# Row sums of an integer softmax on GpSimd, one activation table for Ln and Exp, and a longer run of filler transposes

## The reference, cut to what matters

```python
def _int_log2_softmax(x, scaling_factor):
    ...
    exp_int = jnp.maximum(jnp.floor(z * 2.0 ** (n - q)), 0.0)
    exp_sum = exp_int.sum(axis=-1, keepdims=True)
    ratio = jnp.round(exp_sum / jnp.maximum(exp_int, 1.0))
    ...
    rounds = _log_round(ratio)
    ...
    return jnp.where(mask, 0.0, 2.0 ** (-qlog))
```

```python
k = (x @ w_key.T).reshape(B, S, NH, DK)
v = (x @ w_value.T).reshape(B, S, NH, DV)
gate = jax.nn.sigmoid(x @ w_gate.T)
...
return x + retrieved @ w_out.T
```

## Time and profile before

| | us |
|---|---|
| median of three runs | 588.76 |
| lowest, highest | 588.63, 591.01 |
| the profiled execution | 594.99 |
| its span in the profile | 593.2 |
| TensorE busy | 492.7 (83% of the span) |
| VectorE busy | 319.5 (54%) |
| ScalarE busy | 206.6 (35%) |
| GpSimd busy | 154.6 (26%) |

### The profile page before, as it was taken

The page is one execution under the profiler, slowest core; times in us unless marked ns, Lnnn a source line. Parts: engine busy times, 40 slices in busy tenths (PEclk is TensorE's granted clock), DMA queues, the critical chain, the costliest instruction groups (busy, mean ns, idle before and its releaser), DMA issues.

```text
span 593.2 us, 12427 instructions
## 1 busy us (share of the span) xinstructions
PE 492.7 (83%) x4370; PEld 456.0 (77%) x4371; DVE 319.5 (54%) x1037; ACT 206.6 (35%) x441; POOL 154.6 (26%) x148
## 2 busy tenths in 40 slices
PE   3999999988514676899999679768999999999960
PEld 3999997568513565899999666758999999999950
DVE  1567999778999887322222466793222222222207
ACT  3630013857993357044343152261111121211110
POOL 1493000000001000555533300006544434443120
PEclk9999999989557667799999889879999999999995
DMA  8995100000006422387775497023666556667018
GB/s 302 411 339 152 51 1 1 0 3 2 0 1 220 129 106 108 84 217 179 180 171 109 108 277 306 1 107 98 202 204 184 168 166 187 183 183 209 28 52 294
DMA packets 40659, 84.86 MB, mean 143 GB/s; under 512 B 7270, under 2 KB 23186, under 8 KB 39586
## 3 DMA queue, kind: packets, MB, share of 16 engines
q1 hardware_dynamic: 33218, 72.81, 38.1%
q0 software_dynamic: 7392, 11.41, 8.5%
HBM read 70.33 MB, written 13.86 MB: 142 GB/s over the span
## 4 chain that ended last, share of the span: by engine, by line
PE 69%; DVE 17%; DMA 5%; ACT 4%; issue 2%; SPq 1%; POOL 0%; ACTq 0%; DVEq 0%; POOLq 0%
PE ps L1136 19%; PE ps L1112 13%; PE ps L886 13%; PE ps L1120 7%; DVE h L1923 2%; PE ps L1001 2%; DMA arena<-tok_w 1%; PE ps L1103 1%; PE ps L973 1%; DVE xT L1770 1%; PE ps L974 1%; PE ps L866 1%; PE ps L867 1%; DVE arena L1624 1%; DVE arena L1485 1%
## 5 line engine op out<-in xcount | busy, mean ns | idle before, releaser
L1136 PE MATMUL ps<-arena,xn 128*128 x696 | 123.1, 327 | 2.1 <-ACT xn L776 2.1
L1136 PEld LDWEIGHTS ps<-arena,xn 128*128 128x128 f32 x696 | 111.8, 190 | 4.2 <-issue 3.9
L514 POOL DMA_INDIRECT xT<-rows,from_i x58 | 56.3, 971 | 164.0 <-DVE from_i L1784 118.9
L886 PE MATMUL ps<-arena 128*128 128x192 f32 (+1 forms) x588 | 85.4, 333 | 10.2 <-DMA arena<-x_strips 9.2
L529 POOL DMA_INDIRECT made<-xT,to_i x58 | 67.9, 1170 | 99.2 <-DVE xT L1822 65.7
L886 PEld LDWEIGHTS ps<-arena 128*128 128x128 f32 (+1 forms) x588 | 83.3, 194 | 10.9 <-ACT arena L555 8.9
L1112 PE MATMUL ps<-xn,arena 128*128 128x128 f32 x696 | 88.0, 277 | 0.0
L1112 PEld LDWEIGHTS ps<-xn,arena 128*128 128x128 f32 x696 | 86.1, 194 | 0.1
L779 ACT ACTIVATE xn<-ps 128x384 f32<-128x384 f32 x78 | 32.6, 493 | 141.3 <-PE ps L1122 114.9
L1810 DVE COPY xn<-ps 128x128 f32<-128x128 f32 x58 | 16.9, 292 | 117.2 <-PE ps L1104 114.8
L776 ACT ACTIVATE xn<-ps,b_all 128x128 f32<-128x128 f32 x114 | 30.8, 390 | 62.6 <-PE ps L1122 51.0
(11 more groups left out here) (373 smaller groups left out, 771.1 us busy)
## 6 DMA issues: line engine op xcount, KB each, us to landing
arena<-ffn_a SPq DMA_DIRECT2D x58, 384.0 KB, 3.9
arena<-ffn_b SPq DMA_DIRECT2D x116, 96.0 KB, 4.4
arena<-x_blocks SPq DMA_DIRECT2D x16, 384.0 KB, 6.7
arena<-x_strips SPq DMA_DIRECT2D x3, 1536.0 KB, 12.3
arena<-ffn SPq DMA_DIRECT2D x4, 1152.0 KB, 15.5
rows<-xn SPq DMA_DIRECT2D x8, 384.0 KB, 2.3
arena<-made SPq DMA_DIRECT2D x8, 384.0 KB, 6.2
arena<-tok_w SPq DMA_DIRECT2D x8, 288.0 KB, 7.4
```

Source lines behind the costliest of these rows:

```text
L514: pool.indirect_dma_start(sx[:, k % 6], None, F["src"], bass.IndirectOffsetOnAxis(from_i[:, k:k + 1], 0)).then_inc(sem(f"sx_in{k % 6}"), 16)
L886: mm = pe.matmul(sum_ps(name, j), xs[rows, strip, 2 * j + b, 128 * c:128 * c + 128], w[rows], start=(name, j // 2) not in opened, stop=lef ...
L1136: mm = pe.matmul(ps[:, result_bank(k, N), 0:DIM], hT[:, u % 2, 128 * c:128 * c + 128], F["w2"][:, bass.ds(e2 + DIM * c, DIM)], start=(c == ...
```

## The change

- GpSimd gets a function `row_sums`: for each part it adds the 16 elements of a row by pairs, in four additions (768, 384, 192 and 96 elements in a partition). VectorE's reduction at line 1600 is gone.
- `ratios` no longer overwrites `Ee` in its first two instructions but writes into `quot`, at the place of `wx`; its third instruction waits for `row_sums` and writes `Ee`. So `weights(0)`, which writes `wx`, now waits for the ratios of both parts.
- ScalarE loads the table set `natural_log_exp_and_others` after the scores, ahead of `values(0, 2)`.
- On ScalarE `thirds(0)` moves behind two `on_diagonal`, and `thirds(1)` behind the fourth.
- `keep_clock(18)` in the linear stage becomes `keep_clock(36)`.
- Semaphores are merged: `tok_b_in` into `cst_in` (now 32), `b2_in` into `ffn_in0` (now 32), `ones_row`, `gate_set` and `wnat_set` into `pool_set`, `gate_logit` and `soft_in` into `exp_in`, `gate_exp` and `soft_exp` into `exp_out`.

The diff, without the further lines of the merged semaphores:

```diff
+        quot = view(18432, [3072])
...
-            sp.dma_start(tok_b_row[:], tok_b).then_inc(sem("tok_b_in"), 16)
+            sp.dma_start(tok_b_row[:], tok_b).then_inc(sem("cst_in"), 16)
...
-            sp.wait_ge(sem("cst_in"), 16)
+            sp.wait_ge(sem("cst_in"), 32)
...
-            sp.dma_start(b2_all, ffn0_b2.to_broadcast([128, E0 * DIM])).then_inc(sem("b2_in"), 16)
+            sp.dma_start(b2_all, ffn0_b2.to_broadcast([128, E0 * DIM])).then_inc(sem("ffn_in0"), 16)
...
+            def row_sums(part):
+
+                pool.wait_ge(sem("exp_int"), part + 1)
+                E = Ee[:, 1536 * part:1536 * part + 1536].rearrange("p (a b) -> p a b", b=16)
+                pairs = view(24960, [96, 8])
+                link(pool.tensor_tensor(pairs, E[:, :, 0:8], E[:, :, 8:16], ALU.add))
+                for half in (4, 2):
+                    link(pool.tensor_tensor(pairs[:, :, 0:half], pairs[:, :, 0:half], pairs[:, :, half:2 * half], ALU.add))
+                pool.tensor_tensor(rsum[:, 96 * part:96 * part + 96], pairs[:, :, 0], pairs[:, :, 1], ALU.add
+                                   ).then_inc(sem("row_sums"), 1)
+
+            row_sums(0)
+            pool.wait_ge(sem("row_sums"), 1)
+            row_sums(1)
             pool.wait_ge(sem("o_ps"), 4)
...
             for g in range(4):
                 scores(g)
+            act.preload_act_table_set("natural_log_exp_and_others")
             values(0, 2)
...
-            thirds(0)
             on_diagonal(0, 0)
             on_diagonal(1, 0)
+            thirds(0)
             on_diagonal(2, 0)
+            on_diagonal(3, 0)
             thirds(1)
-            on_diagonal(3, 0)
...
-            keep_clock(18)
+            keep_clock(36)
             pe.wait_ge(sem("near_xn"), 6)
...
             def exponentials(part):
-                c, b = part_of[part]
+                c = part_of[part][0]
                 dve.wait_ge(sem("power_ready"), 2 * part + 2)
                 dve.scalar_tensor_tensor(Ee[:, c], Ee[:, c], k_sq, half_ps[part], ALU.add, ALU.mult).then_inc(sem("exp_int"), 1)
-                dve.wait_ge(sem("exp_int"), part + 1)
-                link(dve.tensor_reduce(rsum[:, b], rows(Ee[:, c]), AX.X, ALU.add))
 
             def ratios(part):
 
-                R = Ee[:, part_of[part][0]]
+                E, R = Ee[:, part_of[part][0]], quot[:, part_of[part][0]]
                 dve.wait_ge(sem("guess"), part + 1)
-                link(dve.scalar_tensor_tensor(R, R, 2.0 ** -30, half_ps[part], ALU.mult, ALU.mult))
+                link(dve.scalar_tensor_tensor(R, E, 2.0 ** -30, half_ps[part], ALU.mult, ALU.mult))
                 link(dve.scalar_tensor_tensor(R, R, 2.0, half_ps[part], ALU.subtract, ALU.mult))
-                dve.scalar_tensor_tensor(rows(R.bitcast(I32)), rows(R), -2.0 ** -30, across(rsum, part), ALU.mult,
+                dve.wait_ge(sem("row_sums"), part + 1)
+                dve.scalar_tensor_tensor(rows(E.bitcast(I32)), rows(R), -2.0 ** -30, across(rsum, part), ALU.mult,
                                          ALU.mult).then_inc(sem("ratio"), 1)
...
                 dve.wait_ge(sem("thirds"), part + 1)
+                if part == 0:
+                    dve.wait_ge(sem("ratio"), 2)
```

More of the change, by code:

```diff
@@ L478, in link @@
                 pool.wait_ge(sem("pool_step"), steps[0])
-            pool.memset(xT1[K1:128, :], 1.0).then_inc(sem("ones_row"), 1)
-            pool.wait_ge(sem("ones_row"), 1)
+            pool.memset(xT1[K1:128, :], 1.0).then_inc(sem("pool_set"), 1)
+            pool.wait_ge(sem("pool_set"), 1)
             link(pool.memset(wnat[96:128, 5:7, :], 0.0))
             for w in gate_w1:
-                pool.memset(w[K1:128], 0.0).then_inc(sem("gate_set"), 1)
-            pool.memset(wnat[64:128, 4, :], 0.0).then_inc(sem("wnat_set"), 1)
-            pool.wait_ge(sem("wnat_set"), 1)
+                pool.memset(w[K1:128], 0.0).then_inc(sem("pool_set"), 1)
+            pool.memset(wnat[64:128, 4, :], 0.0).then_inc(sem("pool_set"), 1)
+            pool.wait_ge(sem("pool_set"), 4)
             pool.wait_ge(sem("w_row"), 1)
@@ L504, in _ @@
                 pool.tensor_tensor(s[:, 0, :], s[:, 0, :], s[:, 2, :], ALU.add).then_inc(sem("w_sums"), 1)
+            def row_sums(part):
[10 more added lines that the diff above has]
+            row_sums(1)
             pool.wait_ge(sem("o_ps"), 4)
-            pool.memset(aqT1[K1:K1 + 3], 1.0).then_inc(sem("ones_row"), 1)
+            pool.memset(aqT1[K1:K1 + 3], 1.0).then_inc(sem("pool_set"), 1)
             def exchange(F):
@@ L809, in _ @@
             ins.then_inc(sem("lin_a"), 1)
-            act.wait_ge(sem("gate_logit"), 1)
-            act.activation(stat[:, 501:502], stat[:, 500:501], ACT.Exp, scale=-1.0).then_inc(sem("gate_exp"), 1)
+            act.wait_ge(sem("exp_in"), 1)
+            act.activation(stat[:, 501:502], stat[:, 500:501], ACT.Exp, scale=-1.0).then_inc(sem("exp_out"), 1)
             transposed(3)
-            act.wait_ge(sem("soft_in"), 1)
+            act.wait_ge(sem("exp_in"), 2)
             d16 = rt[:, 432:448]
-            act.activation(d16, d16, ACT.Exp).then_inc(sem("soft_exp"), 1)
+            act.activation(d16, d16, ACT.Exp).then_inc(sem("exp_out"), 1)
             all_norms(1)
@@ L859, in logits @@
                 if i == 0:
-                    pe.wait_ge(sem("gate_set"), 2)
+                    pe.wait_ge(sem("pool_set"), 3)
                 pe.wait_ge(sem("xT0_ready"), 4 * (1 + 2 * n) + i + 1)
@@ L928, in _ @@
                     if (name, b) == ("m2", 1):
-                        pe.wait_ge(sem("cst_in"), 16)
+                        pe.wait_ge(sem("cst_in"), 32)
                         pe.wait_ge(sem("w_sums"), 2)
-                        pe.wait_ge(sem("tok_b_in"), 16)
                         pe.matmul(ps[:, 4, 0:DIM], ones, sum_g[:, 0, :], start=True, stop=True)
@@ L953, in _ @@
             pe.wait_ge(sem("bias_in"), 16 * BIASES)
-            pe.wait_ge(sem("ones_row"), 1)
+            pe.wait_ge(sem("pool_set"), 1)
             def qk_free(n):
@@ L1061, in _ @@
             pe.wait_ge(sem("aq_act"), 5)
-            pe.wait_ge(sem("ones_row"), 2)
+            pe.wait_ge(sem("pool_set"), 5)
             pe.wait_ge(sem("wp_ready"), 2)
@@ L1172, in experts @@
                 up(1, 1, 0)
-                pe.wait_ge(sem(f"ffn_in{n}"), 16 if n == 0 else 16 * E1 // 2)
+                pe.wait_ge(sem(f"ffn_in{n}"), 32 if n == 0 else 16 * E1 // 2)
                 pe.wait_ge(sem(f"tiles_ready{n}"), 1)
@@ L1347, in _ @@
             dve.wait_ge(sem("blk_read"), 16)
-            dve.wait_ge(sem("cst_in"), 16)
+            dve.wait_ge(sem("cst_in"), 32)
             away, away_sq = stat[:, 100:101], stat[:, 101:102]
@@ L1463, in _ @@
             token_row(1)
-            dve.wait_ge(sem("wnat_set"), 1)
+            dve.wait_ge(sem("pool_set"), 4)
             dve.wait_ge(sem("wnat_in"), 128)
@@ L1735, in route @@
                     link(dve.tensor_tensor(d16, c16, a16, ALU.subtract))
-                    dve.tensor_tensor(d16, d16, stat[:, 464:480], ALU.mult).then_inc(sem("soft_in"), 1)
+                    dve.tensor_tensor(d16, d16, stat[:, 464:480], ALU.mult).then_inc(sem("exp_in"), 1)
                 dve.wait_ge(sem("rank_ps"), n + 1)
@@ L1798, in route @@
                 if n:
-                    dve.wait_ge(sem("soft_exp"), 1)
+                    dve.wait_ge(sem("exp_out"), 2)
                     link(dve.tensor_scalar(c16, d16, 1.0, None, ALU.add))
@@ L1831, in copies @@
                 if n == 0:
-                    dve.wait_ge(sem("b2_in"), 16)
+                    dve.wait_ge(sem("ffn_in0"), 32)
                 dve.wait_ge(sem(f"tiles_ready{n}"), 1)
@@ L1892, in _ @@
             link(dve.tensor_tensor(ltmp[:, 0:16], ps[:, 6, 0:16], cst[:, C_SEL:C_SEL + 16], ALU.mult))
-            dve.tensor_reduce(stat[:, 500:501], ltmp[:, 0:16], AX.X, ALU.add).then_inc(sem("gate_logit"), 1)
+            dve.tensor_reduce(stat[:, 500:501], ltmp[:, 0:16], AX.X, ALU.add).then_inc(sem("exp_in"), 1)
             plus_normed(12, 16)
-            dve.wait_ge(sem("gate_exp"), 1)
+            dve.wait_ge(sem("exp_out"), 1)
             link(dve.tensor_scalar(stat[:, 502:503], stat[:, 501:502], 1.0, None, ALU.add))
```

## The result

| us | before | changed |
|---|---|---|
| median (20 executions each) | 592.72 | 588.56 |
| lowest, highest | 588.63, 596.27 | 586.62, 590.48 |
| the profiled execution | 594.99 | 588.58 |
| its span | 593.2 | 586.8 |

A forecast was written before the change was run, and what follows sets the result against it. The prediction took ScalarE and VectorE, ending together, to bound the softmax and TensorE's clock the linear stage. Softmax 1.9 + fillers 1.3 + semaphores zero = 3.2 us; 588.76 - 3.2 = 585.5 us, range 583.6 to 587.8.

The forecast's parts named there:

- The base: Whole kernel: the median of 588.76 us before the change, from which the summed gain of 3.2 us was taken.
- the fillers bring nothing in most runs: Rival, linear stage: the runs behind the median had no clock fall, so only the softmax's 1.9 counts: 586.9 us; chance 0.23.
- Softmax, ScalarE: Softmax: one hidden table load replaces four, so the first guess comes earlier and VectorE starts 2.45 us sooner.
- Softmax, VectorE and GpSimd: Softmax: reductions leave VectorE, GpSimd sums a part in 4.1 us, in time; the ratios end 1.9 us earlier.
- the term of 0.55 for the meeting: Softmax: VectorE's line 1608 meets GpSimd's second addition of part 1; charged 0.55 us, bounds 0 to 1.8.
- Its new wait for both ratios costs nothing: Softmax: `weights(0)` now waits for the ratios of both parts; claimed cost zero, as VectorE issues it after them.
- GpSimd's third addition waits in turn: Softmax: the addition waits for VectorE's line 1608, but its sum still comes at 165, before it is due at 167.5.
- the term of 1.3: Linear stage: 36 fillers keep TensorE's clock from falling during the products; 1.3 us saved, bounds 0 to 1.65.
- The added ones cost nothing: Linear stage: the 18 added fillers fit into TensorE's wait of 2.12 us for VectorE; uncovered they would cost 2.0 us.
- Merged semaphores: Whole kernel: each merged semaphore waits for a transfer or memset that landed long before; effect zero.
- become the bound: Rival, softmax: GpSimd's sums set the pace and the kernel is slower, 589.5 us at 8.2 a part; chance 0.07.
- the loads stay at Ln and Exp: Rival, softmax: table loads remain, VectorE starts as before and only the fillers count: 587.5 us; chance 0.06.

The follow-up runs named there:

- the bridge: 14 more fillers between the first and second transposed tile of the experts of layer 0, in the kernel before: 591.69 us, ratio 0.9998.
- the set of 12 above: The kernel before, unedited, run again against itself: 591.84 us (588.53 to 594.95) over 12 executions.

## Why the prediction was wrong, point by point

**The base: the step that failed.** The sum ended in "588.76 - 3.2 = 585.5". The mean gain of all executions is 591.94 - 588.53 = 3.4 us, and the ratio of 0.994 is that of the forecast, 0.9945; but the base was 3 us too low. That the gain agrees is in part luck: the softmax gave 0.4 us more than its term and the fillers, in the mean, about 1 less, and some 0.8 of the 3.4 us have no cause here. The three runs of 588.63, 588.76 and 591.01 came from a kernel whose executions go from 588.1 to 598.5 with a median of 591.4 (592.72 in the 20 beside the changed kernel). From 592.72 the sum would give 589.5; the measured 588.56 is 0.9 below that. The sign was there to be seen: the profiled execution lay 6.2 above the median, and I wrote that "the terms are local and carry over". One of them, the fall at the linear stage, was a part of what made that execution long, and couldn't be subtracted from a median of executions without it. The median less the softmax alone would have been consistent: 588.76 - 2.31 = 586.4, about the fastest execution of the changed kernel (586.62), as 588.76 was about the fastest of the one before. The rival "the fillers bring nothing in most runs" had this thought, but kept the base too. The range was too narrow in the same place: it took 0.3 us on the high side from three runs.

**Softmax, ScalarE: right.** First correction 2.51 us earlier against its exponential; forecast 2.45. The one load hides in ScalarE's idle time. A load of 1.28 us is followed by the activation 0.01 to 0.02 later in all rows, so the price of 2.66 us for a switch, which the Trainium skill gives (ScalarE: Activation LUTs, What ACT_TABLE_LOAD costs), is not borne out here. The second guess, no longer late, was worth 0.19 on VectorE's side and not 0.1.

**Softmax, VectorE and GpSimd: right in kind, mis-sized.** The sum was 2.45 - 0.55 = 1.9; the stage's length gave 2.31. By the rows that is 2.51 for the guess, 0.19 for the second guess, less 0.21 for the meeting, less 0.19 ahead of the masks. So the term of 0.55 for the meeting is the mis-sized one. "Its new wait for both ratios costs nothing, since VectorE issues it after them anyway" was wrong as far as the rows tell: with this wait the masks start 1.86 to 1.87 us after the last product, without it 1.67 to 1.68. The two terms of 0.19 cancel by chance. The part on GpSimd was forecast at 4.1 us and took 3.9; the rows of 8, 4, 2 and 1 cost nothing extra: 768 elements took 1.80, 384 and 192 together 1.58, and 96 took 0.36. I had looked for the whole price on VectorE's side; most of it fell on GpSimd, 1.40 us, where there was slack of 2.7 us (its sum was there at 163.54, wanted at 166.23). "GpSimd's third addition waits in turn" was right.

**Linear stage: the term of 1.3 failed too.** What the fall costs was priced right: the products were 1.63 us shorter, of the 1.65 worked out. But even between the two profiled executions the late fillers took 0.91 of it back, so that 0.72 was left. In the mean, 36 in place of 18 fillers is worth 0.3 us in the changed kernel (588.82 - 588.53, with a standard error of 0.55) and 0.0 in the one before. What it does in the changed kernel is to cut the long executions off: none of 32 was above 590.7 us, of those with 18 fillers 7 of 24. In the kernel before it does not. "The added ones cost nothing; the wait of 2.12 us for VectorE covers them" was wrong: in ten profiled executions with 18 fillers the wait was 0.94 to 2.12 us, and in seven of them it was below the 1.96 that the 18 added take. In 5 of 7 profiled executions with 36 TensorE was late, by 0.56 to 0.93 us. "I expect no fall with 36" held in every profile.

**Merged semaphores: zero, as far as the stages show.** All stretches that the stage table doesn't name took 278.15 us together, against 278.03 before, and the means of the kernel with the changed softmax and 18 fillers and of the one before differ by 3.1 us, with a standard error of 0.6, where the softmax explains 2.3. No run took the merging alone.

**Rivals.** GpSimd did not become the bound: its part would have to be about twice as long. That the loads stay at Ln and Exp was not so. "The fillers bring nothing in most runs" is what the medians show, with the softmax at 2.3 instead of 1.9; its 586.9 has the same base, 3 us too low.

**What stays open.** The means leave 3.4 - 2.3 = 1.1 us to the fillers and to what else changed; in the kernel before neither the 36 fillers nor the bridge alone gives anything, and both together remove the long executions. In none of 11 profiled executions with the changed softmax (one of them bridged) did the clock fall in the experts, against 3 of 7 with the old softmax and no bridge. That suggests that the change also took that fall away, by shifting what comes when, but none of 11 beside 3 of 7 would come by chance once in 23 times, and no run showed a mechanism. No version was found that surely beats the changed kernel: with 18 and 26 fillers the medians are lower by 0.4 and 0.1 us, single executions go up to 594, and the means are no better.

## What to carry to other kernels

Before a forecast is subtracted from a median, ask whether the profiled execution and the median are of the same kind: a term that is a part of what made the profiled execution long (a clock that fell) counts only in the share of executions that have it, and three runs do not tell that share. Where two engines end together, price their reliefs as a pair: here 0.24 and -0.20 alone and 2.31 together. And a term read from two profiled executions has to be counted with what the edit costs beside it: the products gained 1.63 us and the late fillers took 0.91 back. Size fillers by the shortest wait they must fit into, not by the wait of one profile.

## What the runs showed of the hardware that was not expected

- When a GpSimd addition and a VectorE instruction with two large inputs in SBUF met, the one that came second paid: 1.62 us for VectorE when it came just after a long addition had started, 0.21 when near its end, and 1.40 for the GpSimd addition that had to wait for VectorE.
- The same code, on one core, takes 588 to 598 us (588.12 to 596.8 within one set of 35), and the granted clock goes with it (correlation -0.83 in the set of 12 above).
- The fall of the clock is not set by the kernel alone: after 26 fillers it fell in one execution and not in another, with the same instructions around it. Without any fillers the low level lasted from 343.8 to 350.6 us in the profiled execution and cost 2.95.
- GpSimd's additions over rows of 8, 4, 2 and 1 elements cost no more than the line through two additions of the patch stage says (1.80, 1.58 and 0.36 us against 1.82, 1.59 and 0.39).
